# Attention part: the context's low parts and the input's addition move from VectorE into accumulating DMAs

## The reference, cut to what matters

```python
# B = 16 samples, T = 112 tokens, C = 256, context of S = 375 rows a sample, H = 16 heads of D = 16
q = softmax(heads(x @ Wq.T + bq), axis=-1)
k = softmax(heads(y @ Wk.T + bk), axis=-1)          # y: the context
v = heads(y @ Wv.T + bv)
D_inv = 1.0 / sum(q * sum(k, axis=-2), axis=-1)
out = q + einsum('bhnd,bhde->bhne', q, einsum('bhnd,bhne->bhde', k, v)) * D_inv
out = out @ Wp.T + bp

x = layernorm(x + rwkv(x))       # the part before
x = layernorm(x + out)           # this part
x = layernorm(x + experts(x))    # the part after
```

## Time and profile before

| | |
|---|---|
| median of 3 runs | 1837.98 us (1837.52 to 1838.78) |
| profiled execution | 1839.21 us, its span 1837.5 us |
| TensorE busy | 1736.6 us, 95% of the span |
| VectorE busy | 1242.6 us, 68% |
| ScalarE busy | 977.0 us, 53% |
| GpSimd busy | 3.6 us |
| mean granted TensorE clock | 0.98 |
| DMA | 56.59 MB, all of it from SP's queue but for instructions |

### The profile page before, as it was taken

One profiled execution on the slowest core, in us unless ns is written; L12 is line 12 of the kernel. 1 busy time (PEld: TensorE's weight loads), 2 busy tenths in 40 slices (PEclk: granted clock), 3 DMA queues, 4 the chain that ended last, 5 costly groups with the idle time before them and its releaser, 6 DMA issues.

```text
span 1837.5 us, 27225 instructions
## 1 busy us (share of the span) xinstructions
PE 1736.6 (95%) x10508; PEld 1520.3 (83%) x10508; DVE 1242.6 (68%) x1918; ACT 977.0 (53%) x1505; POOL 3.6 (0%) x26
## 2 busy tenths in 40 slices
PE   3599999999999998998999999999999999999997
PEld 1378888778888788888899889998999989999896
DVE  7999999999999855888554445444454544445446
ACT  4688898898989773444533333333333332333323
POOL 0000000000000000000000000000000000000000
PEclk9799999999999998999999999999999999999999
DMA  4000010001000002111111010000011001120001
GB/s 143 1 25 17 12 47 18 7 8 62 1 12 29 0 30 89 44 55 45 55 35 35 1 35 35 34 33 2 34 34 34 11 23 34 34 74 0 1 1 41
DMA packets 34702, 56.59 MB, mean 31 GB/s; under 512 B 3030, under 2 KB 20412, under 8 KB 33596
## 3 DMA queue, kind: packets, MB, share of 16 engines
q1 hardware_dynamic: 34620, 55.47, 9.3%
HBM read 51.79 MB, written 3.67 MB: 30 GB/s over the span
## 4 chain that ended last, share of the span: by engine, by line
PE 70%; DVE 24%; ACT 3%; issue 2%; DMA 0%; SPq 0%; ACTq 0%; DVEq 0%
PE fbank L1935 33%; PE fbank L1957 17%; PE pair L839 5%; PE pair L799 4%; PE pair L824 3%; DVE kfl L421 2%; PE proj L1429 2%; PE pair L809 2%; DVE st L268 2%; DVE aa L370 1%; DVE bb L366 1%; DVE pp L352 1%; PE qbanks L1465 1%; PE pair L789 1%; DVE x L409 1%
## 5 line engine op out<-in xcount | busy, mean ns | idle before, releaser
L1757 DVE TENSOR_TENSOR hf<-sil,fbank 128x512 f32<-128x512 f32 (+1 forms) x256 | 158.8, 620 | 479.2 <-PE fbank L1935 407.5
L1862 ACT ACTIVATE sil<-fbank 128x512 f32<-128x512 f32 (+1 forms) x256 | 139.2, 544 | 615.1 <-PE fbank L1935 615.1
L1935 PE MATMUL fbank<-xh,wh 128*128 128x512 f32 (+1 forms) x1024 | 289.8, 364 | 1.2 <-ACT sil L1862 1.2
L1935 PE MATMUL fbank<-xl,wh 128*128 128x512 f32 (+1 forms) x1024 | 289.0, 363 | 0.0
L1935 PE MATMUL fbank<-xh,wl 128*128 128x512 f32 (+1 forms) x1024 | 288.9, 363 | 0.0
L1957 PE MATMUL fbank<-wl,hh 128*128 128x256 f32 x896 | 250.3, 279 | 0.0
L1957 PE MATMUL fbank<-wh,hh 128*128 128x256 f32 x896 | 250.2, 279 | 0.0
L1957 PE MATMUL fbank<-wh,hl 128*128 128x256 f32 x896 | 250.1, 279 | 0.0
L1935 PEld LDWEIGHTS fbank<-xl,wh 128*128 128x128 f32 x1024 | 184.6, 189 | 30.8
L1935 PEld LDWEIGHTS fbank<-xh,wl 128*128 128x128 f32 x1024 | 184.4, 189 | 30.4
L1935 PEld LDWEIGHTS fbank<-xh,wh 128*128 128x128 f32 x1024 | 180.5, 189 | 27.8 <-ACT sil L1862 1.6
(11 more groups left out here) (239 smaller groups left out, 3109.6 us busy)
## 6 DMA issues: line engine op xcount, KB each, us to landing
raw<-in_w_gate SPq DMA_DIRECT2D x16, 512.0 KB, 3.8
raw<-in_w_up SPq DMA_DIRECT2D x16, 512.0 KB, 4.7
raw<-in_w_down SPq DMA_DIRECT2D x16, 512.0 KB, 5.7
raw<-in_w_ck SPq DMA_DIRECT2D x4, 1024.0 KB, 4.8
raw<-in_w_cv SPq DMA_DIRECT2D x4, 1024.0 KB, 4.8
raw<-in_ctx_t SPq DMA_DIRECT2D x4, 750.0 KB, 5.9
ct<-in_ctx_t SPq DMA_DIRECT2D x4, 750.0 KB, 4.9
x<-in_x SPq DMA_DIRECT2D x4, 448.0 KB, 6.9
```

The costliest lines, as they stand in the source:

```text
L1757: dve.tensor_tensor(hf[i][:, 0:w], sil[i][:, 0:w], banks(e, t, f)[1][:, 0:w], ALU.mult).then_inc(hf_ready, 1)
L1862: act.activation(sil[f % 2][:, 0:w], banks(e, t, f)[0][:, 0:w], ACT.Silu).then_inc(sil_ready, 1)
L1935: ins = pe.matmul(banks(e, t, f)[k][:, 0:w], m[h][:, o:o + P], a[:, b, columns(c)], start=i == 0, stop=i == 3 * CB - 1)
```

## The change

Low parts: ScalarE writes minus the high part into `ctl`, right after the high part, and GpSimd issues a DMA that adds the context in HBM to it (`accum_op=ALU.add`, 375 KB). TensorE waits for that DMA (`ctl_in`, one semaphore for each buffer). Input: GpSimd issues a DMA that adds the input chunk in HBM to `x` (448 KB), and VectorE waits for it before the statistics (`input_stats`). `xin` is gone. SP's context loads wait for `cth_ready` in the place of `ctl_ready`. The place of `kvbd` in memory moves, and a memset of GpSimd for the experts waits for `num_done`.

```diff
@@ gpsimd @@
+            def add_context(s):
+
+                pool.wait_ge(minus_ready, s + 1)
+                if s >= 2:
+
+                    pool.wait_ge(ctl_in[s % 2], 16 * (s // 2))
+                pool.dma_start(ctl[s % 2][:, :, 0:S], io["ctx_t"][:, :, s * S:(s + 1) * S].bitcast(F32R),
+                               accum_op=ALU.add).then_inc(ctl_in[s % 2], 16)
+
+            def add_input(c):
+                if c >= 2:
+
+                    pool.wait_ge(sum_in[c % 2], 16 * (c // 2))
+                pool.dma_start(x[:, c * G:(c + 1) * G, :], xv[:, c * G:(c + 1) * G, :], accum_op=ALU.add)\
+                    .then_inc(sum_in[c % 2], 16)
+
+            add_context(0)
+            add_context(1)
+            pool.wait_ge(g["x_done"], 2 * STEPS)
+            add_input(0)
+            for s in range(2, B):
+                add_context(s)
+                if s % 2 == 0 and s // 2 < GROUPS:
+                    add_input(s // 2)
@@ sync @@
             sp.wait_ge(g["x_done"], 2 * STEPS)
-            load_x(0)
-            load_x(1)
             sp.dma_start(g["wrt"][:], io["wrt"]).then_inc(g["wrt_in"], 16)
             load_half(sp, g["raw"][0], io, 0, 0, g["raw_in"][0])
             for j in range(2, B // CG):
 
-                sp.wait_ge(ctl_ready, CG * (j - 1))
+                sp.wait_ge(cth_ready, CG * (j - 1))
                 load_context(sp, io, ct, ct_in, j)
-                if j * CG % G == 0 and j * CG // G >= 2:
-                    c = j * CG // G
-
-                    sp.wait_ge(sum_done, c - 1)
-                    load_x(c)
@@ vector @@
-            def low_context(s):
-
-                c0 = (s % CG) * S
-                dve.wait_ge(cth_ready, s + 1)
-                if s >= 2:
-
-                    dve.wait_ge(proj_done, s - 1)
-                dve.tensor_tensor(ctl[s % 2][:, :, 0:S], ct[s // CG % 2][:, :, c0:c0 + S], cth[s % 2][:, :, 0:S],
-                                  ALU.subtract).then_inc(ctl_ready, 1)
-
...
-            def add_input(c):
-                dve.wait_ge(xin_in[c % 2], 16 * (c // 2 + 1))
-                dve.tensor_tensor(chunk(c), chunk(c), xin[c % 2][:], ALU.add).then_inc(sum_done, 1)
-                dve.wait_ge(sum_done, c + 1)
+            def input_stats(c):
+                dve.wait_ge(sum_in[c % 2], 16 * (c // 2 + 1))
                 stats(1, c)
...
-                low_context(0)
...
-                low_context(1)
...
-                        add_input(c1)
+                        input_stats(c1)
...
-                    if n + 2 < B:
-                        low_context(n + 2)
@@ scalar, high_context @@
                 act.activation(cth[s % 2][:, :, 0:S], ct[s // CG % 2][:, :, c0:c0 + S], ACT.Copy).then_inc(cth_ready, 1)
+                act.wait_ge(cth_ready, s + 1)
+                act.activation(ctl[s % 2][:, :, 0:S], cth[s % 2][:, :, 0:S], ACT.Copy, scale=-1.0).then_inc(minus_ready, 1)
@@ tensor, project @@
-                pe.wait_ge(ctl_ready, s + 1)
+                pe.wait_ge(ctl_in[s % 2], 16 * (s // 2 + 1))
```

More of the change, by code:

```diff
@@ L928, in attention_phase @@
         x, ident = g["x"], g["ident"]
-        xin = [sb(f"xin{i}", [T, G, C]) for i in range(2)]
+        kvbd = sb("kvbd", [P, 2 * G, CB, P])
         q = [sb(f"q{i}", [T, G, C]) for i in range(2)]
@@ L945, in attention_phase @@
         top, total, rec = (sb(n, [ST, STILES * H]) for n in ("top", "total", "rec"))
-        kvbd = sb("kvbd", [P, 2 * G, CB, P])
         kcm = sb("kcm", [P, 2 * G, CB, P // D])
@@ L972, in attention_phase @@
         wkvh_ready, wkvl_ready = sem("wkvh_ready"), sem("wkvl_ready")
-        cth_ready, ctl_ready = sem("acth_ready"), sem("actl_ready")
+        cth_ready, minus_ready = sem("acth_ready"), sem("minus_ready")
+        ctl_in = [sem(f"actl_in{i}") for i in range(2)]
         v01_done, v2_done, proj_done, kv_done = sem("v01_done"), sem("v2_done"), sem("proj_done"), sem("kv_done")
@@ L977, in attention_phase @@
         bd_ready = sem("bd_ready")
-        xin_in = [sem(f"xin_in{i}") for i in range(2)]
-        sum_done = sem("sum_done")
+        sum_in = [sem(f"sum_in{i}") for i in range(2)]
         lnstat, lnlog, lny0, shift_ready = ({i: sem(f"{n}{i}") for i in (1, 2)}
@@ L987, in attention_phase @@
         dve_step = sem("adve_step")
-        g["sum_done"], g["v01_ready"], g["karg_ready"] = sum_done, v01_ready, arg_ready
+        g["num_done"], g["v01_ready"], g["karg_ready"] = num_done, v01_ready, arg_ready
         TURNS = (2 * G + 2, 3 * G + 2)
@@ L1014, in gpsimd @@
                                pattern=[[D, P // D], [0, D]], channel_multiplier=-1).then_inc(mask_set, 1)
+            xv = io["x"].rearrange("b t c -> t b c")
+            def add_context(s):
[17 more added lines that the diff above has]
+                    add_input(s // 2)
         def sync(sp):
-            xv = io["x"].rearrange("b t c -> t b c")
-            def load_x(c):
-                sp.dma_start(xin[c % 2][:], xv[:, c * G:(c + 1) * G, :]).then_inc(xin_in[c % 2], 16)
             sp.wait_ge(g["wo_done"], STEPS)
@@ L1036, in sync @@
             for j in range(2, B // CG):
-                sp.wait_ge(ctl_ready, CG * (j - 1))
+                sp.wait_ge(cth_ready, CG * (j - 1))
                 load_context(sp, io, ct, ct_in, j)
-                if j * CG % G == 0 and j * CG // G >= 2:
-                    c = j * CG // G
-                    sp.wait_ge(sum_done, c - 1)
-                    load_x(c)
             for c in range(GROUPS):
                 if c == 2:
-                    sp.wait_ge(ctl_ready, B - CG)
+                    sp.wait_ge(cth_ready, B - CG)
                     load_half(sp, g["raw"][1], io, 0, 1, g["raw_in"][1])
@@ L1687, in gpsimd @@
         def gpsimd(pool):
-            pool.wait_ge(g["sum_done"], GROUPS)
+            pool.wait_ge(g["num_done"], GROUPS)
             pool.memset(eps[:], EPS).then_inc(eps_set, 1)
```

## The result

The changed kernel takes 1846.85 us (median of 8 runs, 1843.05 to 1848.22), the kernel before, run beside it, 1838.3 us (8 runs, 1836.29 to 1839.11). The ratio is 1.0044, with a 95% interval of 1.0035 to 1.0054: the change makes the kernel 8.5 us slower. The forecast was 1850, slower. Of all runs in this document one lies far off, a run of e2_input at 2032.54 us with a granted clock of 0.819; the ratios leave it out.

A forecast was written before the change was run, and what follows sets the result against it. The prediction took TensorE (95% busy) as the bound, with VectorE also nearly full in attention. Its terms, 4.4 + 4.0 + 1.3 + 0.9 + 1.6 = 12.2 us on 1839.2, gave 1851.4, forecast as 1850; range 1836 to 1872.

The forecast's parts named there:

- the signs that the prediction named: Attention part: waits of several us at samples 5, 9, 12; landings 6 to 9 us; VectorE less busy, ScalarE more.
- one sign of being wrong: Any of: landings under 4 us, waits at nearly every sample, TensorE's clock falling much longer than 3.2 us, VectorE slowed.
- The transfer's price: Low parts: a 375 KB accumulation alone takes 6.5 us, from a plain 750 KB load's 4.9 us plus 1.6 us.
- the company: Samples 5 and 9: SP's context load on the same DMA engines adds 2.5 us to the low part's transfer.
- the three terms: TensorE's project at samples 5, 9 and 12: late low parts cost 4.4, 4.0 and 1.3 us.
- The first chunk: Input chunk 0: its accumulation lands at 712.5 and costs 0.9 us, bounds -2.1 and +1.9 us.
- The break-even of 711.6 us: Input chunk 0: landing at 711.6 costs nothing, since an addition and a subtraction are gone behind it on VectorE.
- The clock: TensorE: the new stalls of samples 5 and 9 bring one more fall of the clock, 1.6 us.
- ScalarE at nothing: ScalarE: 16 minus copies, 13.1 us in all, cost nothing because idle time before v_out hides them.
- The ceiling of VectorE's relief: Attention part: removing VectorE's subtractions and additions gives at most 0.9 + 0.9 + 1.0 + 2.1 = 4.9 us.
- The fourth term: First chunk: ScalarE's normalising stands behind one VectorE addition and one subtraction; removing them gives at most 2.1 us.
- The quick one: Low-part transfers take about 3 us, so nothing new is late and the kernel takes 1833.5 us; chance 0.12.

The follow-up runs named there:

- e2_input: The changed kernel with VectorE's subtraction for the low parts put back, so only the input is added by DMA: 1838.72 us.
- e5_three_buffers: The changed kernel with three buffers in place of two for the high and the low parts: 1833.42 us.
- e12: The changed kernel with three buffers for high and low parts, and SyncE's loads held until the first input chunk is in: 1828.06 us.
- e10: The changed kernel with SyncE's router-weight load and the five loads behind it held until the first input chunk is in: 1839.33 us.
- e3_load_behind: The changed kernel with SyncE's context loads held until the accumulating transfer they ran beside (samples 5 and 9) is in: 1840.41 us.
- e11: The changed kernel with SyncE's loads held behind the first input chunk, and context loads behind the accumulating transfers they would run beside: 1836.84 us.
- e1: The kernel before with only the low parts made by ScalarE and accumulating DMA, the input's addition staying on VectorE: 1847.87 us.
- e9: The changed kernel with a subtraction of the same shape, which nothing waits for, put back on VectorE in 14 groups: 1848.57 us.
- e7: The changed kernel with three buffers for high and low parts and the low parts subtracted on VectorE, input still by DMA: 1839.22 us.
- e13: The changed kernel with three buffers, low parts subtracted on VectorE, and SyncE's loads held behind the first input chunk: 1835.93 us.
- e4_plain_copy: The changed kernel with the low parts' DMA copying instead of adding, so the output is not the reference's: 1836.79 us.

## Why the prediction was right, and where its sizes were off

**The mechanism was right.** In the changed kernel TensorE waits for the low part at project(5), project(9) and project(12) and at no other by more than 0.2 us (its weight load stops for 0.18 us in front of project(4)). These are the samples that the prediction found by the lack of a q or output projection between the keys and the project. e5_three_buffers shows that it is the lead of the chain: with one sample more of it these waits are gone and the same transfers are a gain; e12 against e10 shows it again. Of the signs that the prediction named, the place of the waits, the work of the engines and the attention part as the place of the loss came true. The waits are 2.1 to 2.3 us and not several, the landings 5.0 to 7.3 us (median 5.6) and not 6 to 9, and one sign of being wrong showed: the clock fell for 6.8 us at 796, about twice the 3.2 us.

**The transfer's price was too high.** The step "I add 1.6 us for the second pass and GpSimd's way of issuing, a choice, and take 6.5 us alone" gave 6.5 us; the transfer alone landed after 5.0 us, and from the minus copy's end to project's first matmul it is 5.4 us at sample 12. 5.0 us is 0.1 us over the plain load of 750 KB of the earlier trace rows, so the row of twice the bytes was the price, without the addend. "I add half of the load's 4.9 us, 2.5 us" for the company gave 2.5 us; e3_load_behind shows 0.9 and 0.8 us, e11 against e10 1.7 and 1.3 us. So the three terms 4.4 + 4.0 + 1.3 = 9.7 us measured 2.6 + 1.2 - 0.5 = 3.3 us (with the waits that they absorb: 1.15 us behind sample 9, 2.9 us behind sample 12).

**The first chunk** was put at 0.9 us, with bounds of -2.1 and +1.9. In the profiled run it is 1.2 us, with VectorE's statistics at 714.45. The size is near by luck: the chunk was later than priced (10.5 us from issue to landing), the turn of its tokens came 2.1 us later, and 0.9 us of that came back by where the clock was low. Alone the chunk takes 5.7 us (e10) and not 7.5, and the company costs it 4.8 us and not 2. The break-even of 711.6 us counts the subtraction that is gone; but before, that subtraction stood behind the keys of sample 0 (714.32, the keys at 713.45), so for the keys, the statistics' 710.77 of before is the break-even, and these keys are what TensorE waits for longest. With the chunk early the turn comes 2.1 us sooner than before (e10 and e11), which is the lower bound; the other 0.4 us that e10 is ahead at project(2) are the clock's. The wait on SyncE that ensures this is worth 4.2 us up to the turn in the traces and 7.5 us of the median, nearly the whole 8.5. The prediction treated this term as a small one beside three large ones; for the median it is as large as they are.

**The clock** was put at one more fall, 1.6 us. It measured -1.5 + 2.7 + 1.6 = 2.8 us: the fall at 741 didn't come, the stall of sample 9 brought one of 6.8 us, and the one behind the attention part was longer. (The 0.9 us that the clock gave back at the first chunk stand in that term.) That such falls go with stalls was right. That their number can be counted from the stalls was not: the stall of 2.28 us before 753.32 brought none, one of 4.26 us at the same place in e1 did.

**The sum.** 3.3 + 1.2 + 2.8 = 7.3 us of terms against 12.2 forecast; 0.7 us ahead of the change and 0.5 us at the end make the 8.5. So the transfers were priced 6.4 us too high, the clock 1.2 us and the first chunk 0.3 us too low, and 1.2 us at the two ends had no term. That the forecast came within 3.2 us owes something to luck: the errors go against each other.

**ScalarE at nothing** fits what the traces show, though no experiment added the copies alone. With the minus copies project(0) starts at 700.78 (e9), 700.88 (e3) and 700.89 (e5), but also at 701.94 (e10) and 701.98 (e1); without them at 700.88 (before), 699.79 (e7) and also 701.91 (e2). So the changed kernel's 0.7 us lie within what differs between runs of either kind.

**The ceiling of VectorE's relief**, 0.9 + 0.9 + 1.0 us at samples 9 to 13 of its 4.9, measured 0.8 + 0.8 + 1.0 in e12 against e13. The fourth term, 2.1 us at the first chunk, is the 2.1 us by which the turn comes sooner in e10 and e11.

**The rivals.** The quick one said 1833.5 us for transfers of about 3 us. e4_plain_copy comes near to these, 3.5 us at best and 3.9 in the median, but 4.6, 4.7 and 3.8 us at samples 5, 9 and 12. It takes 1836.79 us, with the first chunk late and three waits of 0.6 to 0.9 us left, so the rival's price was roughly right and its condition false. The Trainium skill ("DMA: Bandwidth & Descriptors", "Anatomy of one DMA — SWDGE (gpsimd) path") gives an estimate of 2.9 us for such a copy, with which this first rival would have come true (the prediction says the second by a slip). The copy landed after 3.5 us at best and the accumulation after 5.0; the measurement decides. Of the blocking of GpSimd's descriptors by VectorE, which the Trainium skill states too ("SBUF — State Buffer", "SBUF: two separate sides"), nothing shows: the 14 issue instructions of low parts behind 700 us took 1.05 to 1.10 us each, in a part in which VectorE is busy most of the time. That does not test the rule, since no trace shows whether any VectorE instruction beside them used such a mode, and no run here took VectorE's work away from beside them.

## What to carry to other kernels

An engine's work given to a DMA is not shorter, only elsewhere: here 0.93 us on VectorE became 0.83 us on ScalarE and over 5 us of latency, and it paid only when the buffers gave the chain one step more of lead (from 8.5 us slower to 4.8 us faster). A transfer that a full engine's queue waits for should be alone: one wait on the queue of the other loads was worth 7.5 us of the median (the traces show 4.2 us of it, up to the turn of the first chunk), and in e10's trace TensorE has no new wait by it. And before you buy such a lead, look which transfer stands in front of the first consumer: its arrival can differ by chance from run to run, and a version that keeps such a wait, as e7 did, tells little of what else it changes.

## What was not expected of the hardware

- An accumulating DMA of 375 KB costs 1.5 us more than a copying one (5.0 against 3.5 us at best), and lands after about as long as a plain load of twice the bytes (4.9 us). The issuing instruction is 1.05 to 1.10 us against 0.70 to 0.72 us.
- SyncE's issue of w_gate, the same instruction at the same place, took 0.44 us in some traces (changed, e4, e7, e9) and 1.33 to 1.75 us in others (e2, e3, e5), always beside GpSimd's issue of the first chunk. With 0.44 us the statistics started 9.3 to 10.5 us after the chunk's issue, with 1.33 to 1.75 us after 6.3 to 8.8 us. That the slow issue lets the chunk through first is what this looks like, and e10 fits it; why the issue is slow, no run tells.
- The clock's falls are not settled by the program. In e10 and e11 TensorE waits 1.78 us and comes to the keys of sample 0 at 714.28 and 714.32, and then it runs at half clock for 10.2 us in one and 3.4 us in the other. Project(2) comes 2.9 us sooner in e11, with hardly another difference between the two up to there. The stretches of e10_input_first and, below it, e11_both_holds (granted clock 0.61 and 0.87):

```profile
714.00:727.00 13.00, 11.06 (x44) 8.95 (x45) 5.79 (x14) 5.27 (x8) 1.09 (x1) 0.61 1.06 261
```

```profile
714.00:727.00 13.00, 11.21 (x68) 10.08 (x69) 8.06 (x15) 5.95 (x10) 1.09 (x1) 0.87 0.99 221
```

TensorE is busy for the same 11 us in both, with 44 matmuls done at a granted clock of 0.61 and 68 at 0.87. Spreads of 5 us and more between runs of one version, as here, can come from this alone, and a single trace should be read with it in mind.
